# Gate rows by DMA, basis units between the convolution's stages, three heads on GpSimd, and a wait for ScalarE in one fused graph kernel

## The reference, cut to what matters

```python
h = relu(layernorm(x)); x = x + attention_layer(h)   # 8 heads of 64, masked by the adjacency, softmax over queries
h = relu(layernorm(x)); x = x + gin_layer(h)         # lin, then twice: aggregate, W1, prelu, W2, batch norm
h = relu(layernorm(x)); x = x + gcn_layer(h)         # normalised aggregate of h @ W
h = relu(layernorm(x)); x = x + rgcn_gate(h)         # two relational layers
# attention: q, k, v = h @ W; s = q k^T / 8, masked; p = softmax(s, axis=nodes); o = p v @ Wo
#   h1 = ln(h + o); y = ln(h1 + relu(h1 @ W1 + b1) @ W2 + b2)
# rgcn layer: w[r] = sum_b att[r, b] * basis[b]      (2 relations, 30 bases of 512 x 512)
#   out = sum_r segment_sum(sigmoid(x @ gate_w[r]) * x @ w[r]) + x @ root + bias
```

## Time and profile before

| what | value |
|---|---|
| median of three timed executions | 470.44 us (468.74 to 473.02) |
| profiled execution, its own time | 473.26 us |
| span of that execution in the profile | 471.5 us |
| TensorE (PE) busy | 444.5 us, 94% |
| VectorE (DVE) busy | 345.0 us, 73% |
| ScalarE (ACT) busy | 243.7 us, 52% |
| GpSimd (POOL) busy | 51.1 us, 11% |
| mean granted TensorE clock | 0.989 of full |

### The profile page before, as it was taken

One profiled execution on the slowest core, in us unless ns is written; L12 is line 12 of the kernel. 1 busy time (PEld: TensorE's weight loads), 2 busy tenths in 40 slices (PEclk: granted clock), 3 DMA queues, 4 the chain that ended last, 5 costly groups with the idle time before them and its releaser, 6 DMA issues.

```text
span 471.5 us, 6210 instructions
## 1 busy us (share of the span) xinstructions
PE 444.5 (94%) x2214; PEld 276.5 (59%) x2214; DVE 345.0 (73%) x725; ACT 243.7 (52%) x425; POOL 51.1 (11%) x60
## 2 busy tenths in 40 slices
PE   2999999999888799989999999999989999999996
PEld 1443433444333234767868677678657688888885
DVE  4987877799999777966877784757687776675212
ACT  4888784586697622744224535545572443511210
POOL 3200000044444330100001000000000000000000
PEclk9999999999999799989999999999999999999999
DMA  7984544304999996955339949570797722000002
GB/s 262 400 361 151 206 116 158 108 0 177 384 422 376 377 373 222 378 179 213 114 112 388 417 154 370 189 289 2 279 366 221 283 95 92 3 0 2 0 3 89
DMA packets 18458, 98.17 MB, mean 208 GB/s; under 512 B 3711, under 2 KB 4095, under 8 KB 7935
## 3 DMA queue, kind: packets, MB, share of 16 engines
q1 hardware_dynamic: 14439, 73.38, 41.1%
q0 software_dynamic: 3552, 24.12, 13.7%
q10 hardware_dynamic: 432, 0.20, 0.2%
HBM read 92.45 MB, written 5.24 MB: 207 GB/s over the span
## 4 chain that ended last, share of the span: by engine, by line
PE 76%; DVE 19%; ACT 2%; issue 2%; DMA 1%; DVEq 0%; ACTq 0%
PE bank L1259 16%; PE sbank L1582 9%; PE bank L1330 7%; PE sbank L1245 7%; PE bank L1595 6%; PE sbank L1313 6%; PE bank L1477 5%; PE bank L1567 5%; DVE s L937 4%; PE bank L1297 3%; PE sbank L1438 3%; PE sbank L1227 2%; DVE softmax_tmp L862 2%; DVE s L962 2%; DVE sum_tmp L948 2%
## 5 line engine op out<-in xcount | busy, mean ns | idle before, releaser
L758 DVE TENSOR_SCALAR cnt<-iota_row,edge_f 128x512 bf16<-128x512 f16 x132 | 41.2, 348 | 5.6 <-PE sbank L1313 5.6
L1245 PE MATMUL sbank<-bring,attw 120*32 120x512 f32 x320 | 38.9, 599 | 0.3 <-DMA bring<-in_basis 0.3
L1330 PE MATMUL bank<-hT,wring 128*128 128x512 f32 x64 | 31.2, 633 | 0.2 <-ACT hT L422 0.2
L1313 PE MATMUL sbank<-cnt,adjT 128*128 128x512 bf16 x132 | 30.3, 381 | 0.0
L499 ACT ACTIVATE adjT<-distance,edge_w,edge_f 128x128 bf16<-128x128 bf16 x61 | 29.2, 479 | 1.4 <-PE sbank L1313 1.4
L410 ACT ACTIVATE stat<-stat,eps 128x1 f32<-128x1 f32 x32 | 9.3, 295 | 39.2 <-DVE stat L764 39.2
L1245 PE MATMUL bank<-bring,attw 120*32 120x512 f32 x192 | 24.6, 624 | 3.8 <-DMA bring<-in_basis 3.7
L1176 DVE SCALAR_TENSOR_TENSOR y_lo<-sbank,gate,y_hi 128x512 fp32r<-128x512 f32 x16 | 11.8, 749 | 22.2 <-ACT y_hi L685 22.2
L1259 PE MATMUL bank<-hT_hi,w_hi 128*128 128x512 f32 x64 | 26.2, 410 | 1.7 <-DVE y_hi L996 1.7
L438 ACT ACTIVATE s<-bank,colsb 128x512 f32<-128x512 f32 x24 | 16.4, 686 | 20.9 <-PE bank L1259 20.9
L755 DVE TENSOR_SCALAR adjT<-iota_row,edge_f,edge_w 128x128 bf16<-128x128 f16 x71 | 22.0, 310 | 6.4 <-PE sbank L1313 6.4
(11 more groups left out here) (225 smaller groups left out, 1064.2 us busy)
## 6 DMA issues: line engine op xcount, KB each, us to landing
bring<-in_basis SPq DMA_DIRECT2D x63, 1024.0 KB, 7.7
wring<-in_weights POOLq DMA_DIRECT2D x8, 1024.0 KB, 9.2
landing<-in_weights POOLq DMA_DIRECT2D x4, 1024.0 KB, 7.7
w_scratch<-stage SPq DMA_DIRECT2D x64, 64.0 KB, 7.7
hT<-in_weights POOLq DMA_DIRECT2D x4, 1024.0 KB, 7.6
qkw<-w_scratch POOLq DMA_DIRECT2D x2, 2048.0 KB, 8.2
rring<-in_rows POOLq DMA_DIRECT2D x12, 256.0 KB, 8.0
xr<-in_x SPq DMA_DIRECT2D x4, 256.0 KB, 4.8
```

The lines of the kernel that those rows point to most:

```text
L758: dve.tensor_scalar(hot_s[:, n % HOT, :], iota[:, :], src_f[:, n:n + 1], None, ALU.is_equal).then_inc(sem("hot_ready"), 1)
L1245: mm = pe.matmul(unit_bank(b)[32 * j:32 * j + 32, :], attw[0:KB, u // UNITS, g, :], bring[0:KB, u % BATCH, j, :], start=(g == 0), stop=(g ...
L1313: pe.matmul(bank[7][:, :], hot_d[:, n % HOT, :], hot_s[:, n % HOT, :], start=(n == 0), stop=(n == ECH - 1)).then_inc(sem("hot_used"), 1)
L1330: mm = pe.matmul(bank[at][:, :], a, b, start=(k == 0), stop=(k == C - 1))
```

## The change

Five edits, in one diff:

1. **Heads.** OWN_HEADS is 5, so VectorE multiplies five heads (1280 columns) and GpSimd three (768). GpSimd's sum_heads goes; VectorE adds heads 0 to 3 to heads 4 to 7 in one instruction of 1024 columns, then halves twice more.
2. **Gate rows.** The products on PE and the copies on ScalarE go. GpSimd gathers the four rows from the column table into scratch space in device memory (four DMAs of 512 single elements), early, and broadcasts them into hT once c2_1's parts are made, ahead of root1's load. SP waits for them before it stores the last batch over that scratch space.
3. **Units.** One unit moves from step 6 of the attention loop to step 0; two now stand ahead of c2_1 instead of behind, three behind it, none between the gcn aggregate and gcn, and one instead of two after rel_root(0, 0). The numbers on ScalarE follow. So that bank 2 is free for step 0, v's tiles 1 to 3 all use bank 3 (v_bank).
4. **Feed-forward buffers.** f1a and f2a land in landing, f1b and f2b in hT; f1a's load is now the early one, and f1b's comes behind the attention loop.
5. **f1b.** Its tiles wait for ScalarE having taken the bank (T_hi) and no longer for VectorE (ff1). VectorE's additions that make adj go behind each of the four parts of f2b.

```diff
@@ -74,16 +74,16 @@
 SLOTS = 3
-OWN_HEADS = 6
+OWN_HEADS = 5
 EARLY_UNITS = 8
-STEP_UNITS = (0, 2, 3, 3, 3, 3, 4, 2)
+STEP_UNITS = (1, 2, 3, 3, 3, 3, 3, 2)
 ATTENTION_BATCHES = (EARLY_UNITS + sum(STEP_UNITS)) // BATCH + 1
-PLACE = {"q": 0, "k": 1, "v": 2, "o": 3, "f1a": "hT", "f1b": "landing", "f2a": "hT", "f2b": "landing", "lin": 3,
+PLACE = {"q": 0, "k": 1, "v": 2, "o": 3, "f1a": "landing", "f1b": "hT", "f2a": "landing", "f2b": "hT", "lin": 3,
          "c1_0": 1, "c2_0": "hT", "c1_1": "landing", "c2_1": "hT", "gcn": "landing", "root1": 2,
@@ -93,7 +93,7 @@
 IN_PARTS = tuple(PARTS)
-LAST_READ = {"f1a": ("v_psum", C), "f1b": ("q_psum", C), "f2a": ("weight_parts", C),
+LAST_READ = {"f1a": ("q_psum", C), "f1b": ("v_psum", C), "f2a": ("weight_parts", C),
              "f2b": ("weight_parts", 2 * C), "c1_0": ("ff1_psum", C), "lin": ("ff1_psum", 2 * C),
@@ -212,12 +212,14 @@
 packed = adjT[:, 3, :].bitcast(I32)
-pool_tmp = adjT[:, 0, :].rearrange("p (a n) -> p a n", a=2)
+four_sums = adjT[:, 0:2, :].rearrange("p c (a n) -> p (c a) n", a=2)
 digits = s01[:, :, :].bitcast(I32)
     return colsb[:, at + i:at + i + n]
+gate_scratch = scratch[1, UNITS - BATCH, 0:2 * RELS, :]
@@ -236,9 +238,9 @@
 if name == "f2a":
-    return xT_lo, hT_r
+    return xT_lo, y1_lo
 if name == "f2b":
-    return w0_hi, y1_lo
+    return w0_hi, hT_r
 return ((w0_hi, w0_lo), (w1_hi, w1_lo))[PARTS[name][0]]
@@ -254,6 +256,10 @@
     return bank[(2 if b < ATTENTION_BATCHES else 6) + b % 2]
+def v_bank(c):
+    return 3 if c else 2
@@ -303,6 +309,8 @@
 layer, g = divmod(b, BATCHES)
+if b == 2 * BATCHES - 1:
+    sp.wait_ge(sem("gate_rows"), 16 * 2 * RELS)
 for j in range(COLT):
@@ -359,7 +367,12 @@
-load_weight("f1b")
+for i in range(2 * RELS):
+    at = COLS[f"gw{i // RELS + 1}"][0]
+    pool.dma_start(gate_scratch[i, :].rearrange("(k p) -> p k", p=P),
+                   cols[:, at:at + RELS * C].rearrange("p (k r) -> p r k", r=RELS)[:, i % RELS, :],
+                   allow_slow_non_contiguous=True).then_inc(sem("gate_rows_gathered"), 16)
+load_weight("f1a")
@@ -368,24 +381,12 @@
-def sum_heads(it):
-    sc = probs_of(it)
-    pool.wait_ge(sem("exped"), 2 * it + 1)
-    pool.tensor_tensor(pool_tmp, sc[:, 0:2, :], sc[:, 2:4, :], ALU.add).then_inc(
-        sem("pool_sum"), 1)
-sum_heads(0)
 scale_heads(0)
-sum_heads(1)
 scale_heads(1)
-sum_heads(2)
-load_weight("f1a")
 load_row("g2", "v")
     scale_heads(it)
-    if it + 1 < 2 * C:
-        sum_heads(it + 1)
+load_weight("f1b")
 load_weight("f2a")
@@ -396,8 +397,15 @@
 load_row("bias2", "x_plus")
-for n in ("c2_0", "c1_1", "c2_1", "gcn", "root1"):
+for n in ("c2_0", "c1_1", "c2_1", "gcn"):
     load_weight(n)
+pool.wait_ge(sem("gate_rows_gathered"), 16 * 2 * RELS)
+pool.wait_ge(sem("weight_parts"), (IN_PARTS.index("c2_1") + 1) * C)
+for i in range(2 * RELS):
+    pool.dma_start(gate_rows[:, i, :], gate_scratch[i, :].partition_broadcast(P)).then_inc(
+        sem("gate_rows"), 16)
+load_weight("root1")
 load_w(0)
@@ -640,10 +648,7 @@
 batch_norm(1, 3)
-stage_units(2)
-for i in range(2 * RELS):
-    act.wait_ge(sem("gate_rows_psum"), i + 1)
-    act.copy(gate_rows[:, i, :], bank[4 + i % 2][:, :]).then_inc(sem("gate_rows"), 1)
+stage_units(5)
@@ -656,12 +661,10 @@
     act.copy(x_hi[:, c, :], hr[:, c, :]).then_inc(sem("h_gcn_hi"), 1)
-    if c == 0:
-        stage_units(4)
+stage_units(4)
 for c in range(C):
 split_weight("root1")
-stage_units(2)
@@ -707,11 +710,10 @@
 rel_turn(0, 1)
-stage_units(2)
 root(7, 2)
 rel_turn(0, 2)
-stage_units(2)
+stage_units(3)
 root(7, 3)
@@ -778,7 +780,7 @@
 dve.wait_ge(sem("v_psum"), c + 1)
-dve.tensor_tensor(vr[:, c, :], bank[2 + c % 2][:, :], row("bv"), ALU.add).then_inc(sem("v"), 1)
+dve.tensor_tensor(vr[:, c, :], bank[v_bank(c)][:, :], row("bv"), ALU.add).then_inc(sem("v"), 1)
@@ -945,9 +947,8 @@
 dve.wait_ge(sem("exped"), 2 * it + 2)
-after(step(dve.tensor_tensor(sum_tmp[:, :, :], sc[:, 4:6, :], sc[:, 6:8, :], ALU.add)))
-dve.wait_ge(sem("pool_sum"), it + 1)
-after(step(dve.tensor_tensor(sum_tmp[:, :, :], sum_tmp[:, :, :], pool_tmp, ALU.add)))
+after(step(dve.tensor_tensor(four_sums, sc[:, 0:4, :], sc[:, 4:8, :], ALU.add)))
+after(step(dve.tensor_tensor(sum_tmp[:, :, :], four_sums[:, 0:2, :], four_sums[:, 2:4, :], ALU.add)))
 if it:
@@ -986,10 +987,6 @@
 split_weight("f2a")
-for c in range(C):
-    after(step(dve.tensor_tensor(adj[:, c, :], cnt[:, 0, c, :], cnt[:, 1, c, :], ALU.add)))
-    dve.tensor_tensor(adj[:, c, blk(P, c)], adj[:, c, blk(P, c)], ident[:, :],
-                      ALU.add).then_inc(sem("adj"), 1)
@@ -1006,6 +1003,9 @@
     split_weight("f2b", (c,))
+    after(step(dve.tensor_tensor(adj[:, c, :], cnt[:, 0, c, :], cnt[:, 1, c, :], ALU.add)))
+    dve.tensor_tensor(adj[:, c, blk(P, c)], adj[:, c, blk(P, c)], ident[:, :],
+                      ALU.add).then_inc(sem("adj"), 1)
 for c in range(C):
@@ -1160,7 +1160,7 @@
 for rel in range(RELS):
-    dve.wait_ge(sem("gate_rows"), layer * RELS + rel + 1)
+    dve.wait_ge(sem("gate_rows"), 16 * 2 * RELS)
     for c in range(C):
@@ -1238,8 +1238,10 @@
     pe.wait_ge(sem("stage_ready"), b - 1)
-if g == 0 and 0 <= b - EARLY_UNITS // BATCH < 2:
-    pe.wait_ge(sem("v"), 3 + b - EARLY_UNITS // BATCH)
+if g == 0 and b == EARLY_UNITS // BATCH:
+    pe.wait_ge(sem("v"), 1)
+elif g == 0 and b == EARLY_UNITS // BATCH + 1:
+    pe.wait_ge(sem("v"), C)
 pe.wait_ge(sem(f"basis{u % BATCH}_loaded"), 16 * (u // BATCH + 1))
@@ -1263,7 +1265,7 @@
-def parts_stage(wname, x, ready, done, order=None, t_major=True):
+def parts_stage(wname, x, ready, done, order=None, t_major=True, taken=None):
@@ -1272,6 +1274,8 @@
     seen = need
+if taken and k == 0:
+    pe.wait_ge(sem("T_hi"), T_ORDER.index(taken) * C + c + 1)
 mm = parts_tile(x, weight_parts(wname), c, k, t_major)
@@ -1322,8 +1326,8 @@
 elif which:
-    pe.wait_ge(*((sem("v"), c - 1) if c >= 2 else (sem("k"), C)))
-at = 2 + c % 2 if which == 2 else c
+    pe.wait_ge(*((sem("v"), c) if c >= 2 else (sem("k"), C)))
+at = v_bank(c) if which == 2 else c
 for k in range(C):
@@ -1465,7 +1469,7 @@
 parts_stage("f1a", hT_parts, None, "ff1_psum", order=BY_TILE)
-parts_stage("f1b", hT_parts, "ff1", "ff1_psum", order=BY_TILE)
+parts_stage("f1b", hT_parts, None, "ff1_psum", order=BY_TILE, taken="ff1")
 units(2)
@@ -1525,22 +1529,10 @@
 parts_stage("c1_1", hT_parts, "agg1", "c1_1_psum")
+units(2)
 parts_stage("c2_1", x_parts, "c1_1", "c2_1_psum")
-units(2)
-def gate_row(i):
-    if i >= 2:
-        pe.wait_ge(sem("gate_rows"), i - 1)
-    for k in range(C):
-        mm = pe.matmul(bank[4 + i % 2][:, blk(P, k)],
-                       col(f"gw{i // RELS + 1}", k * RELS + i % RELS).to_broadcast([P, P]),
-                       ident[:, :], start=(k == 0), stop=(k == C - 1), skip_group_check=True)
-    mm.then_inc(sem("gate_rows_psum"), 1)
-need_parts("c2_1")
-gate_row(0)
-gate_row(1)
+units(3)
 pe.wait_ge(sem("c2_1"), C)
@@ -1549,13 +1541,10 @@
             mm.then_inc(sem("x4_psum"), 1)
-gate_row(2)
-gate_row(3)
 units(4)
 aggregate("h_gcn_parts", "agg2_psum", order=ALL_BANKS)
-units(2)
 parts_stage("gcn", hT_parts, "agg2", "gcn_psum", t_major=False)
@@ -1614,7 +1603,7 @@
 rel_root(0, 0)
-units(2)
+units(1)
 turn_rel(0, "h_rel0", 2)
```

## The result

| | before | after |
|---|---|---|
| median of the timed executions | 470.47 us (20: 468.74 to 473.24) | 468.53 us (20: 467.48 to 470.02) |
| profiled execution, its own time | 473.26 us | 467.95 us |
| span | 471.5 us | 466.1 us |
| mean granted TensorE clock, profiled | 0.989 | 0.989 |

The ratio of the two is 0.9949, 95% interval [0.9933, 0.9964]: 1.9 us faster by the medians, 2.4 by the ratio, with an interval of 1.7 to 3.2. That is about half of the 4.1 forecast, and within one per cent. Between the two profiled executions it is 5.3 us, more than was forecast. Most of what follows is about that difference.

A forecast was written before the change was run, and what follows sets the result against it. TensorE, busy 444.5 of 471.5 us, was taken as the bound, with VectorE pacing the softmax loop. Terms -1.9, -4.1, +0.1, +1.8 sum to -4.1: 473.26 to 469.2, less 2.8 for the median, 466.3 us; range 461 to 471.

The forecast's parts named there:

- rival C: Softmax loop gains nothing because the DMA rings or ScalarE pace it as VectorE did: 468.2 us; chance 0.20.
- A: Ahead of the second aggregate the rings are quick enough, so x5 sets its start: 463.8 us; chance 0.20.
- B: TensorE's clock holds at the end of attention, saving 2.8 us more: 463.5 us; chance 0.12.
- Attention loop, -1.9: Softmax loop: new row sum and smaller VectorE multiply bring attend(6) 1.9 us earlier.
- step 4: Softmax loop step: maximum waits about 1.0 us for ScalarE, GpSimd's multiply ends 0.5 late; steps 3 and 4 together gain 0.15.
- f1b, -4.1: First feed-forward product: f1b no longer waits for VectorE and ends 4.1 us earlier, some 1.8 of it clock.
- Convolution, +0.1 and +1.8: Around the second aggregate: gate rows and unit order cost 0.1 us net, half clock while idle 1.8 more.
- Slow clock at the loop's end: At attend(6), TensorE waits 3.0 us in one piece for VectorE; the clock of 0.50 stays, no gain counted.
- the last one of the sum: Whole kernel: profiled execution lies 2.8 us above the timed median; that difference is carried over, 469.2 becoming 466.3.
- x5's chain, 11.4: Behind c2_1: the chain making x5 would let the second aggregate start 11.4 us after c2_1.
- D: Softmax loop: GpSimd's 768-column multiply costs much more than 1.92 us, making the kernel slower, up to 480 us; chance 0.06.

The follow-up runs named there:

- heads_alone: Kernel before with only the softmax edit (five heads on VectorE, three on GpSimd, row sum on VectorE), units and loads unmoved: 468.78 us, ratio 0.997.
- f1b_alone: Kernel before with only f1b's tiles waiting for ScalarE's copy and the adj sums moved behind the f2b parts: 468.31 us, ratio 0.9939.
- root1_later: Changed kernel with root1's load asked for when the parts of the second aggregate's input are done, not right after c2_1: 467.06 us.
- before_again: The kernel before, unchanged, run once for a second profile: 472.31 us.
- both_later: Changed kernel with root1's load after the second aggregate's input parts and unit 60 moved behind gcn: 467.68 us.
- root1_mid: Changed kernel with unit 60 behind gcn and root1's load asked for when unit 59 is done: 465.34 us, ratio 0.9886 to the kernel before.

## Why the prediction was right or wrong

**The number.** 466.3 was forecast, 468.53 measured, inside the range of 461 to 471. It lies at the 468.2 of rival C, whose mechanism is refuted below. In the chances, what the text puts below 465.7 (A, B and a third of the forecast) adds up to 0.46, not 0.42.

**Attention loop, -1.9: right.** VectorE's seven steps take 61.6 us in place of 63.8, -2.2. The pieces came as forecast: L950 1.22, the multiply 1.48 (1.46), GpSimd's 768 columns 1.82 (1.92), a wait of 0.94 (1.0) and a collision of 0.41 (0.5) in step 4, which took 9.86 us where 9.4 was named. The loop up to project(0) is 2.0 us shorter than an unchanged one at full clock (69.1 to 67.1), and 3.4 shorter than the profiled one (70.5), which lost more clock. heads_alone shows that 1.1 of the 2.0 need the moved units and loads, which I had named only as cover for the waits for bases.

**f1b, -4.1: right for the profiled execution, too much for the median.** The stretch went from 26.1 to 22.1. But the term held 1.8 us of half clock, which before loses in some executions only. Without it the wait is worth 2.4, and f1b_alone gained 2.2.

**Convolution, +0.1 and +1.8: right, with the clock lost in another place.** 73.2 to 75.4 in the two profiles is +2.2 (forecast +1.9). The basis of unit 60 landed 13.6 us after c2_1 (forecast 13.5). The aggregate started at 15.7, not 14.4, since that unit then ran at half clock, 1.94 us in place of 0.93: 1.0 of the 1.8 put down for the clock was lost there. From its start to gcn the aggregate took 8.2 us, where it took 7.57 before: 0.7. Three units waited for a basis, 5.2 us in all ("2 to 5" was forecast). That bases and root1's load share the rings was right and is shown by root1_later. Against before_again, with half clock in its own aggregate (74.8), the loss is 0.6 in the first profile of the changed kernel and 1.7 in the second. The rate in this stretch was 426 GB/s in 338 to 342 us, as in the earlier trace rows.

**Slow clock at the loop's end, left as it was: half wrong.** It is there in both profiles of the changed kernel, so rival B is refuted. But before loses it there only in some executions: f1b_alone, with the same code up to there, has clock 1.00 in that window, and 11 of the 74 executions of before have a mean clock of 1.000.

**The step that failed** is the last one of the sum: the profiled execution "lies 2.8 above the median of the timed runs, 470.44, and I carry the difference over". The 2.8 us were not an offset. By the table this execution lost 1.4 us at the loop's end (70.5 against 69.1 in f1b_alone) and 1.6 between f1a and f1b (26.1 against 24.4 in heads_alone) that others keep, and it kept 1.6 in the convolution that before_again lost (73.2 against 74.8). So the 1.8 of clock in the f1b term was subtracted from a median that, by the 2.2 that f1b_alone gained, hardly contained it. And the changed kernel has half clock at the loop's end in both its profiles, so carrying the 2.8 over took off a loss that it does have.

From an execution of before that loses the clock in its aggregate alone, as the usual one seems to, the terms measured are -2.0 for the loop, -2.4 for f1b and +0.6 or +1.7 for the convolution. The +1.7 is from the profile with a mean clock of 0.985, which 24 of the 32 executions of the changed kernel have. With it the sum is -2.7, inside the interval of -1.7 to -3.2; with +0.6 it is -3.8, outside. Which stretches the median execution of before loses clock in, and so the last microsecond, isn't settled.

**Rivals.** A is refuted as it stood (5.2 us of waits for bases), though its number for x5's chain, 11.4, was right: both_later and root1_mid start the aggregate at 11.5. C and D are refuted: the loop gained, and GpSimd's multiply took 1.82 us. It took long only in the last step, beside VectorE's own (3.11 us).

## What to carry to other kernels

Before adding up terms from one profile, compare its mean clock and time with the timed executions. If it belongs to a slower group, find the stretches that make it so and keep them out of the terms; they are not an offset that can be carried over. Where several transfers share the rings, the place of a load has two ends: root1's load was too early behind c2_1, where it held up the bases, and too late behind the aggregate's input, where ScalarE's list stood before it. With unit 60 behind gcn in all three, the place between beat both (465.3 us against 466.9 and 467.7). And 3.78 us of products taken from the front of the aggregate bought no earlier start here, since the last basis that it was made to wait for landed 13.6 us after c2_1.

## What the hardware showed that was not expected

Nearly equal waits lead to different clocks. In before, waits of 1.30 and 1.47 us around one unit were followed by 3.68 us for attend(6); in f1b_alone, with the same code there, waits of 1.30 and 1.76 were followed by 1.95, and the window has clock 1.00. The wait between f1a and f1b was followed by half clock in both profiles of before and by full clock in heads_alone. One long wait lost it every time: behind 3.08 to 3.10 us in one piece attend(6) took 2.72 to 3.61 us in each of six profiles, in place of 1.95. Six profiles aren't a rule, and what decides between the cases isn't shown. One program thus has groups of executions whose medians are 4.3 us apart (468.8 and 473.1), with the same code.
